# Low-rank attention: one product for the compressed queries and keys, values turned from the stored keys

## The reference, cut to what matters

```
c_q = h_t @ W_DQ + b_DQ                       # 128 -> 32
c_kv = h_t @ W_DKV + b_DKV                    # 128 -> 32
q_c, k_c, v_c = c_q @ W_UQ + b_UQ, c_kv @ W_UK + b_UK, c_kv @ W_UV + b_UV   # 8 heads x 128
q_r = c_q @ W_QR + b_QR                       # 8 heads x 32
k_r = h_t @ W_KR + b_KR                       # 32, shared by the heads
scores = concat(q_c, q_r) @ concat(k_c, k_r).T / sqrt(160)
o = softmax(scores) @ v_c
return o @ W_O + b_O
```

## Time and profile before

| | |
|---|---|
| median of 3 runs | 1860.89 us (1859.77 to 1863.96) |
| the profiled execution | 1859.78 us |
| its span, first to last instruction | 1858.0 us |
| PE busy | 1735.8 us, 93% |
| DVE busy | 1392.0 us, 75% |
| POOL busy | 1177.4 us, 63% |
| ACT busy | 1114.2 us, 60% |
| mean granted TensorE clock | 0.960 |

### The profile page before, as it was taken

How to read it: one execution, slowest core, us unless ns; L and a number is a source line. 1 busy time by engine, 2 the same in 40 slices (tenths; PEclk the granted TensorE clock), 3 DMA queues, 4 the chain that set the end, 5 groups by cost and what they waited for, 6 DMA issues and landing times.

```text
span 1858.0 us, 40395 instructions
## 1 busy us (share of the span) xinstructions
PE 1735.8 (93%) x15489; PEld 1275.7 (69%) x15489; DVE 1392.0 (75%) x2975; ACT 1114.2 (60%) x2102; POOL 1177.4 (63%) x907
## 2 busy tenths in 40 slices
PE   5689999999877999999999999999999999999995
PEld 4568888888765666666766766666676666677674
DVE  5556777666577877878788788788887878878862
ACT  5446666666575465666566566565656756656662
POOL 4300110010165397898898888889889888888893
PEclk8889999999978899999999999999999999999998
DMA  4555566663000000000001001001001000100101
GB/s 121 137 138 149 151 153 160 161 152 93 28 1 1 1 10 7 10 7 10 8 8 20 7 10 18 9 9 19 10 7 21 7 10 7 19 10 10 19 10 29
DMA packets 198615, 81.56 MB, mean 44 GB/s; under 512 B 152553, under 2 KB 177429, under 8 KB 198293
## 3 DMA queue, kind: packets, MB, share of 16 engines
q1 hardware_dynamic: 198420, 78.98, 18.8%
HBM read 39.83 MB, written 29.88 MB: 38 GB/s over the span
## 4 chain that ended last, share of the span: by engine, by line
PE 55%; DVE 10%; POOL 1%; issue 1%; ACT 1%; DMA 0%; SPq 0%; POOLq 0%
PE pair L1825 12%; PE pair L1876 11%; PE pair L1880 11%; PE pair L1934 11%; DVE amax L1833 4%; PE pair L1927 4%; PE pair L1642 2%; PE pair L1633 1%; DVE o_inv L1944 1%; PE pair L1683 1%; POOL w_mix L1905 1%; DVE stats L486 1%; PE pair L1669 1%; PE pair L1656 1%; DVE q_low L1750 1%
## 5 line engine op out<-in xcount | busy, mean ns | idle before, releaser
L1891 ACT ACTIVATE prob<-pair 128x512 f32<-128x512 f32 x1024 | 604.2, 598 | 444.1 <-PE pair L1880 371.9
L1833 DVE TENSOR_REDUCE amax<-pair 128x1 f32<-128x512 f32 x1024 | 671.0, 683 | 145.1 <-PE pair L1825 142.8
L1825 PE MATMUL pair<-key_hl,q_hi 128*128 128x512 f32 x1024 | 444.5, 437 | 10.0 <-DVE amax L1833 6.9
L1876 PE MATMUL pair<-q_hi,key_hl 128*128 128x512 f32 x1024 | 406.9, 397 | 2.6 <-ACT prob L1891 2.6
L1880 PE MATMUL pair<-q_low,key_h 65*128 65x512 f32 x1024 | 407.3, 398 | 0.0
L1905 POOL TENSOR_TENSOR w_mix<-w_mix,prob 128x1024 f32<-128x1024 f32 x160 | 382.5, 2391 | 24.4 <-ACT prob L1891 7.6
L1905 POOL TENSOR_TENSOR Wm<-Wm,prob 128x1024 f32<-128x1024 f32 x155 | 369.7, 2385 | 21.8 <-ACT prob L1891 5.7
L521 POOL TENSOR_SCALAR veps<-mv 128x8 f32<-128x8 f32 x47 | 11.4, 243 | 473.3 <-DVE mv L494 472.5
L1825 PEld LDWEIGHTS pair<-key_hl,q_hi 128*128 128x128 f32 x1024 | 196.8, 193 | 117.5 <-issue 54.1
L1934 PE MATMUL pair<-prob,values 128*32 128x256 f32 x4096 | 250.7, 386 | 0.0
L1177 DVE TENSOR_REDUCE mx_neg<-pair 128x4 f32<-128x512 f32 x256 | 164.8, 686 | 99.6 <-PE pair L1081 99.5
(11 more groups left out here) (208 smaller groups left out, 2327.6 us busy)
## 6 DMA issues: line engine op xcount, KB each, us to landing
rows_mem<-once SPq DMA_DIRECT2D x128, 128.0 KB, 2.0
queries<-rows_mem SPq DMA_DIRECT2D x64, 256.0 KB, 4.6
keys<-rows_mem SPq DMA_DIRECT2D x16, 1024.0 KB, 6.9
rows_mem<-once SPq DMA_DIRECT2D x128, 64.0 KB, 1.9
q_low<-shift_cols SPq DMA_DIRECT2D x512, 0.5 KB, 2.0
yT<-o_norm SPq DMA_DIRECT2D x256, 32.0 KB, 1.9
x<-x_dram SPq DMA_DIRECT2D x8, 512.0 KB, 7.3
out_dram<-x SPq DMA_DIRECT2D x7, 512.0 KB, 4.0
```

Of the source, the lines that this page charges most:

```text
L1825: e.matmul(row_bank(("row", r, i)), q_hi[:, k, t * P:(t + 1) * P], key_hl[:, b % 2, i * HALF:(i + 1) * HALF], start=True, stop=True, skip_ ...
L1833: e.tensor_reduce(amax1[:, u % 2, t, i:i + 1], row_bank(("row", r, i)), AX_X, ALU.max).then_inc(*row_maxed.up((r, i)))
L1876: e.matmul(bank(j), key_hl[:, b % 2, ks], q_hi[:, k, sl], start=True, stop=False, skip_group_check=True)
L1891: e.activation(prob1[:, g % P_BUFS, half * HALF:(half + 1) * HALF], bank(K_BANKS[(2 * g + half) % 3]), ACT.Exp, scale=SCALE1).then_inc(*ke ...
```

## The change

1. **One product per half.** The items "cq" and "key" become one item "low" with four parts. Its weights are W_DKV, W_KR, W_DQ and W_DQ side by side (128 columns), so that one fp32 product of 128 x 512 gives the keys in partitions 0 to 63 and the compressed queries twice in 64 to 127.
2. **High parts.** In the item's second step ACT writes the high parts of the queries (64 partitions, before 96) and of the keys (64 partitions, before 128) from PSUM. Before, the keys' step also wrote `key_h1` from PSUM; now a fourth step copies it from `key_hl`, in SBUF.
3. **Low parts.** In the third step DVE writes both low parts, one after the other, after both high parts: the queries' into partitions 64 to 95, reading the high part in 32 to 63; the keys' into 64 to 127, reading PSUM and the high part in 0 to 63. Bank 7 is free after both (`keys_done`). The key scores of a batch's first step wait for `key_h1`.
4. **Values.** The bias product and the eight fp32 products from `yT` are replaced by eight fp32r products of a key tile of `key_hl` with `both_parts` (128 x 32, two stacked identities: high part plus low part, bias included). They wait for the second half's `keys_done`.
5. **The plan.** `prepare` has six items instead of eight: low on r = 26 and 30, const on 34, value on 38, nothing on 42 and 46. During batch 0: low on 18 and 22, const 26, value 30. In the hand-interleaved opening the two "low" items stand where "cq" stood, on PE, ACT and DVE, with part 4 where "key" stood on ACT; const and value take banks 2 and 3 after "turn".

The core of the diff:

```diff
     def prepare(b):
-        return ([(kind, b, i) for kind in ("turn", "cq", "key") for i in range(2)]
+        return ([(kind, b, i) for kind in ("turn", "low") for i in range(2)]
                 + [("const", b, 0), ("value", b, 0)])
...
-            elif kind == "cq":
+            elif kind == "low":
                 e.wait_ge(*featured.at(("m", a, 1)))
-                e.matmul(bank(j)[0:QR, :], w_dq, yT[:, a % 2, W + i * HALF:W + (i + 1) * HALF], start=True, stop=True,
-                         skip_group_check=True).then_inc(*cq_done.up((a, i)))
-            elif kind == "key":
-                e.matmul(bank(j), w_keys, yT[:, a % 2, W + i * HALF:W + (i + 1) * HALF], start=True, stop=True,
-                         skip_group_check=True).then_inc(*key_done.up((a, i)))
+                e.matmul(bank(j), w_low, yT[:, a % 2, W + i * HALF:W + (i + 1) * HALF], start=True, stop=True,
+                         skip_group_check=True).then_inc(*low_done.up((a, i)))
...
-                v_bank = bank(j)[:, 0:NT * DC].rearrange("p (t c) -> p t c", t=NT)
-                e.matmul(v_bank, ones_row[:, :], b_dkv.unsqueeze(1).broadcast_to([1, NT, DC]), start=True,
-                         stop=False, skip_group_check=True)
+                e.wait_ge(*mla_built.at("both"))
+                e.wait_ge(*keys_done.at((a, 1)))
                 for t in range(NT):
-                    ins = e.matmul(v_bank[:, t], yT[:, a % 2, W + t * P:W + (t + 1) * P], w_keys[:, 0:DC], start=False,
-                                   stop=True, skip_group_check=True)
+                    ins = e.matmul(bank(j)[:, t * DC:(t + 1) * DC], key_hl[:, a % 2, t * P:(t + 1) * P], both_parts[:, :],
+                                   start=True, stop=True, skip_group_check=True)
...
-            elif kind == "cq" and part == 2:
-                e.wait_ge(*cq_done.at((a, i)))
+            elif kind == "low" and part == 2:
+                e.wait_ge(*low_done.at((a, i)))
                 if a >= 2:
                     e.wait_ge(*query_done.at((NH * (a - 1) - 1, 1)))
-                e.activation(cq[0:QR, a % 2, sl], bank(j)[0:QR, :], ACT.Identity, bias=b_dq).then_inc(
-                    *cq_hi_done.up((a, i)))
-            elif kind == "key" and part == 2:
-                e.wait_ge(*key_done.at((a, i)))
-                if a >= 2:
                     e.wait_ge(*key_scored.at((64 * (a - 1) - 1, 1)))
-                e.activation(key_h1[0:KR, a % 2, sl], bank(j)[0:KR, :], ACT.Identity, bias=b_keys[0:KR])
-                e.activation(key_hl[:, a % 2, sl], bank(j), ACT.Identity, bias=b_keys).then_inc(*key_hi_done.up((a, i)))
+                e.activation(cq[0:KR, a % 2, sl], bank(j)[KR:P, :], ACT.Identity, bias=b_low[KR:P])
+                e.activation(key_hl[0:KR, a % 2, sl], bank(j)[0:KR, :], ACT.Identity, bias=b_low[0:KR]).then_inc(
+                    *low_high_done.up((a, i)))
+            elif kind == "low" and part == 4:
+                e.wait_ge(*low_high_done.at((a, i)))
+                e.activation(key_h1[0:KR, a % 2, sl], key_hl[0:KR, a % 2, sl].bitcast(F32), ACT.Copy).then_inc(
+                    *key_h1_done.up((a, i)))
...
-            elif kind == "cq" and part == 3:
-                rows = slice(DC, 2 * DC)
-                e.wait_ge(*cq_hi_done.at((a, i)))
-                e.scalar_tensor_tensor(out=cq[rows, k, sl], in0=bank(j)[rows, :], scalar=b_dq[rows],
-                                       in1=cq[rows, k, sl].bitcast(F32), op0=ALU.add, op1=ALU.subtract).then_inc(
+            elif kind == "low" and part == 3:
+                e.wait_ge(*low_high_done.at((a, i)))
+                e.scalar_tensor_tensor(out=cq[KR:QR, k, sl], in0=bank(j)[KR:QR, :], scalar=b_dq[DC:KR],
+                                       in1=cq[DC:KR, k, sl].bitcast(F32), op0=ALU.add, op1=ALU.subtract).then_inc(
                     *cq_ready.up((a, i)))
-            elif kind == "key" and part == 3:
-                rows = slice(KR, P)
-                e.wait_ge(*key_hi_done.at((a, i)))
-                e.scalar_tensor_tensor(out=key_hl[rows, k, sl], in0=bank(j)[rows, :], scalar=b_keys[rows],
-                                       in1=key_hl[rows, k, sl].bitcast(F32), op0=ALU.add, op1=ALU.subtract).then_inc(
+                e.scalar_tensor_tensor(out=key_hl[KR:P, k, sl], in0=bank(j)[0:KR, :], scalar=b_low[0:KR],
+                                       in1=key_hl[0:KR, k, sl].bitcast(F32), op0=ALU.add, op1=ALU.subtract).then_inc(
                     *keys_done.up((a, i)))
```

More of the change, by code:

```diff
@@ L234, in low_rank_plan @@
     U = B * NH
-    PARTS = {"query": 3, "turn": 2, "cq": 3, "key": 3, "const": 2, "value": 2, "proj": 2, "quant": 2,
+    PARTS = {"query": 3, "turn": 2, "low": 4, "const": 2, "value": 2, "proj": 2, "quant": 2,
              "product": 2}
@@ L258, in low_rank_plan @@
     opening = {"bias": [((("bias", 0, 0), None, None), 1)]}
-    for item, j in zip(prepare(0), (2, 3, 4, 5, 2, 3, 2, 3)):
+    for item, j in zip(prepare(0), (2, 3, 4, 5, 2, 3)):
         run = begin(item, j)
@@ L369, in build_program @@
         wv = cut(P)
-        w_dq = cut(QR)
-        w_keys = cut(P)
-        b_keys = cut(1)
+        w_low = cut(P)
+        b_low = cut(1)
         w_ffn = cut(C)
@@ L1348, in pe_layers @@
                     pe_turn(e, "b", i + 1)
-                else:
-                    for (item, j, before), part in opening_m["turn" if i == B - 1 else "key"]:
+                elif i == B - 1:
+                    for (item, j, before), part in opening_m["turn"]:
                         pe_low_part(e, item, j, before, part)
@@ L1362, in pe_layers @@
                 elif i == B - 1:
-                    for (item, j, before), part in opening_m["cq"]:
+                    for (item, j, before), part in opening_m["low"]:
                         pe_low_part(e, item, j, before, part)
@@ L1372, in act_layers @@
                 if i == B:
-                    for (item, j, before), part in opening_m["cq"]:
-                        act_low_part(e, item, j, before, part)
+                    for (item, j, before), part in opening_m["low"]:
+                        if part < 4:
+                            act_low_part(e, item, j, before, part)
                 if i >= 2:
@@ L1383, in act_layers @@
                 else:
-                    for (item, j, before), part in opening_m["turn" if i == B - 1 else "key"]:
-                        act_low_part(e, item, j, before, part)
+                    for (item, j, before), part in opening_m["turn" if i == B - 1 else "low"]:
+                        if i == B - 1 or part == 4:
+                            act_low_part(e, item, j, before, part)
                 if i == 2:
@@ L1873, in pe_key_scores @@
             j = K_BANKS[n % 3]
+            if u % NH == t == half == 0:
+                e.wait_ge(*key_h1_done.at((b, 1)))
             if n >= 3:
@@ L2043, in dve_low_weights @@
                 e.wait_ge(*mla_product.at("bias"))
+                e.tensor_tensor(both_parts[:, :], eye[:, 0:DC], eye[:, KR:KR + DC], ALU.add).then_inc(
+                    *mla_built.up("both"))
                 e.tensor_copy(w_out[:, :, :], out_b[:, 0:2 * C].rearrange("p (g c) -> p g c", g=2)).then_inc(
@@ L2203, in shape_constants @@
             np.where(rows // DC == 1, -1.0, 0.0)[:, None],
-            np.where((rows // DC == 2) | (rows == QR + 1), -1.0, 0.0)[:, None],
+            np.where((rows // DC == 1) | (rows == QR + 1), -1.0, 0.0)[:, None],
             np.full((P, 1), -2.0 ** -27),
```

20 lines of the change are left out of this document (8 added, 12 removed).

## The result

The changed kernel takes 1830.59 us (median of 4 runs, 1827.54 to 1832.03) against 1860.33 us for the kernel before (4 runs, 1857.09 to 1863.96): a ratio of 0.9837 with a 95% interval from 0.9815 to 0.986. It is faster, by 1.6%; the difference is small, but the interval excludes no change. The forecast was 1828 us, range 1820 to 1844.

A forecast was written before the change was run, and what follows sets the result against it. PE was taken to bound the kernel. From 1859.8 us: -27.5 (PE) + 4.8 (DVE, ACT) + 1.0 (const's bank) - 1.5 (opening) - 9.5 (clock) = -32.7, so 1827.1, as a median 1828 us; range 1820 to 1844.

The forecast's parts named there:

- PE's items are paid in full: Low-rank heads: helper items add their whole PE time to a 16.64 us floor; 3.93 us less per preparation, 27.5 for seven.
- the bound of 1.98: New value item on PE: upper bound in us if each fp32r product cost as much as both fp32 passes; 0.95 taken.
- The clock: Clock falls during or just after four of seven value items were to vanish with the shorter item: 9.5 us gained.
- The new pairs of low parts: Two DVE instructions in one step at r = 28 and 32: 0.76 us in each of six preparations, 0.2 in batch 0.
- at r = 28 I cost it at nothing: First pair: DVE's 0.76 us delay was to be covered, as the scale then waits 0.76 us less for POOL.
- 0.76 us at r = 32: Second pair: DVE works without a gap, so PE's query product was to start 0.76 us later.
- 0.15 us at const: Const item at r = 34: its bank waits for `q_low`, 0.15 us each, 1 us in all.
- ACT: High-part copy ahead of `q_hi` at r = 29 and 33: up to 0.6 us wait, counted once with r = 32's 0.76.
- The opening: Batch 0's value item 2.9 us shorter, less 1.43 us for keys' low parts ahead of the scaling: 1.5 us gained.
- The clock did not fall elsewhere: Rival that clock falls stay or move, with 9.5 us kept or lost again elsewhere: 1838 us, chance 0.20.
- The low parts were not stretched: Rival that new low-part instructions wait for POOL, 1.84 us more each, 52 us in all: 1880 us, chance 0.05.
- DVE did not become the bound: Rival that DVE bounds heads 3 and 4, waits costing 12.7 instead of 4.6 us: 1836 us, chance 0.10.

The follow-up runs named there:

- experiment 1: The kernel before with the new value item alone, its plan, cq and key items kept: 1837.3 us against 1861.35, ratio 0.987.
- experiment 2: The changed kernel with the old value item (bias product and sixteen fp32 passes): 1845.28 us, ratio 0.9922 to the kernel before.
- experiment 3: The changed kernel with each of the eight new value products issued three times, same result: 1848.08 us, ratio 0.9935 to the kernel before.
- experiment 4: The changed kernel with the quantisation's steps 8 to 13 (maxima, scale) at r = 34 to 47 instead of 30 to 41: 1825.67 us, ratio 0.9812.
- experiment 5: The changed kernel with ACT's copy of the keys' high parts one step later (r = 30 and 34): 1829.95 us, ratio 0.9847 to the kernel before.
- experiment 6: The changed kernel with DVE's low parts of batch 0 behind the last quantised batch's scaling: 1829.25 us, ratio 0.9845 to the kernel before.
- experiment 9: The changed kernel with later copy, other opening order, quantisation's steps spread in batches 1 to 6, next batch's aggregate later: 1817.21 us, ratio 0.9772.
- experiment 8: Both kernels run again unaltered: the kernel before 1860.47 us (one run), the changed kernel 1829.55 us against 1858.57, ratio 0.9845.

## Why the prediction was right

The time is 2.6 us from the forecast, and both causes that it named are shown; the size of the clock's part and the sum for the opening owe something to luck.

- **PE's items are paid in full.** Shown: heads 4 and 5 (experiments 1 and 2). Const and value left head 5 and it came down to 16.65 us. The new value item costs 0.89 us; 0.95 was taken, and the bound of 1.98 was far off. One price was misread: the second key item, at r = 38, cost 1.07 us and not 1.13, and both prices hold a wait. The key item at r = 34 stood 0.41 us behind its neighbour, where 0.23 is the distance without a wait; an item of the same kind that waits for nothing costs 0.87 us ("low" at r = 26).
- **The clock.** Shown as far as the length of the sparse stretch goes: with the old item four and six falls in two profiles and two with the shorter plan (experiment 2), with its short form none behind it in any profile (63 items in nine profiles), with the short form made long again two (experiment 3). That the size of the term, 9.5 us, was right is partly luck of one profile, but the second has 9 us too. What stays open is why the old plan had falls more often than the shorter one. In batches 1 to 6 they follow 8 of 12 long items at r = 46 and 3 of 12 at r = 38; in batch 0 they follow both at r = 38 and one of two at r = 30.
- **The new pairs of low parts.** The steps of the plan gained 18.8 us without the clock; 27.5 - 4.8 - 1.0 = 21.7 were forecast. The mis-sized term is that of the waits: 1.2 us in each of batches 1 to 6 in place of 0.9, and 1.6 us in batch 0 (1.2 by the second profiles of both kernels) in place of 0.2. Its step "at r = 28 I cost it at nothing" failed. The cover that I named exists, since the scale shrank from 2.02 to 1.35 us, but it stands at r = 32, and PE waits ahead of it: at r = 28 for bank 7, and at r = 30 for `q_low`, which stands in DVE's queue behind the pair and ahead of the scale. Head 3 therefore pays 0.82 us, about the 0.78 us that the added instruction takes on DVE. Of this, 0.48 us go when the block maxima leave that queue (experiment 4), and 0.34 us stay, with the wait at r = 28 unchanged. In head 4 I had put 0.76 us at r = 32 and 0.15 us at const. There the cover worked: the distance at r = 32 grew by only 0.09 us. But head 4 should have shrunk by 0.47 us, since by the prices read its items cost 0.89 and 0.91 us in place of 2.27, and it shrank by 0.05. The 0.4 us between are the 0.09, the misread 0.06 of the second key item, and 0.26 at const, which costs 1.17 us at r = 34: like the key item that stood there it starts 0.41 us behind its neighbour, and so takes over its wait. Over both heads the waits are 1.2 us where I had 0.9.
- **ACT** was counted once and costs nothing in the six batches (experiment 5), 0.3 us once in batch 0. **The opening** gave 1.8 us, 1.5 were taken. The value item is 2.9 us shorter, as I had it; the loss of 1.43 us that I set against it is not where I said (experiment 6), and about 1 us is lost with the old items too (experiment 1). The sum is right by luck, and one part of it is not understood.
- **Rivals.** The clock did not fall elsewhere. The low parts were not stretched: 743 to 746 ns for the keys', 748 to 750 for the queries', 16 each. The Trainium skill ("SBUF — State Buffer", "Who interferes with whom") says that a DVE instruction with at most one SBUF input outside the 2-port modes does not contend with GpSimd; the trace agrees. DVE did not become the bound, but in head 3 it is what PE waits for above its own work (experiments 4 and 5). For heads 0 and 2 experiment 9 shows only that the new order takes 0.5 us from each; it moved several steps at once. POOL's 14.9 us of work in a head, which I gave with the earlier trace rows, is that of head 6 of batch 1; those rows show 16.05 to 18.40 us.

## What to carry to other kernels

Where one engine is busy through a stage, price each item by the distance between its neighbours' starts, and read the same stretch with and without the item; that gave PE's terms here within a tenth of a microsecond. Ask of each distance whether it holds a wait: the key item's did, and the item that took its place inherited it. When two small instructions are merged into one step, ask first who waits for the buffer that they hold, in that very step, and whose work stands between them and the idle time that is to cover them: an idle time further down the queue covers only what stands behind it. And count the clock: a sparse item of 2.6 us cost up to 1.5 or 3 us more than its own time, and that part was about a third of the whole gain.

## What the runs showed of the hardware

- Eight fp32r products of 128 x 128 with 32 columns took 0.89 us, eight with 8 columns 0.91 us: here the width cost nothing. Eight fp32 products with 32 columns, sixteen instructions, took 1.98 us, a little over twice as much.
- The granted clock fell from 2.4 to 1.2 GHz during or behind stretches of 2.6 to 2.7 us of products with 32 columns, in 2, 2, 4 and 6 of 7 cases, and in none of 63 with stretches of 0.9 us. In the head of experiment 8 whose clock fell, PE was busy for 21.67 of 21.67 us: it had not been idle before the fall. A fall of 3.4 us cost 1.54 us.
- A tensor_scalar on 128 x 32 elements in SBUF takes 0.18 us in the earlier layer. At r = 32 of batches 1 to 6, beside POOL's sums, it takes 1.99 to 2.15 us in the kernel before and 1.32 to 1.35 us in the changed one, and at r = 40 (experiment 4) 0.42 to 0.44 us.
